# Row statistics of x shared between VectorE and ScalarE, the second source tile from VectorE, eight warming products in place of ten

## The reference

```python
h = jnp.maximum(_layernorm(x, axis=-1), 0.0)      # m, v = mean(x), var(x); (x - m) / sqrt(v + eps)
x = x + _L0_gnn_ref(h, edge_index, ...)           # three edge convolutions, concat @ Wf + bf
h = jnp.maximum(_layernorm(x, axis=-1), 0.0)
x = x + _L1_gnn_ref(h, edge_index, edge_weight, 625, ...)
```

## Time and profile before

| | us |
|---|---|
| three runs | 111.28, 110.65, 111.09 |
| median | 111.09 |
| the profiled execution, whole | 111.21 |
| its span, first to last instruction | 109.4 |

### The profile page before, as it was taken

The page is one execution under the profiler, slowest core; times in us unless marked ns, Lnnn a source line. Parts: engine busy times, 40 slices in busy tenths (PEclk is TensorE's granted clock), DMA queues, the critical chain, the costliest instruction groups (busy, mean ns, idle before and its releaser), DMA issues.

```text
span 109.4 us, 2712 instructions
## 1 busy us (share of the span) xinstructions
PE 98.6 (90%) x1050; PEld 91.8 (84%) x1050; DVE 87.9 (80%) x257; ACT 63.8 (58%) x154; POOL 20.8 (19%) x27
## 2 busy tenths in 40 slices
PE   0395999979999999999999999999999999999950
PEld 0333898867799989999999999999999999999840
DVE  2589999999999998999953599940999989808960
ACT  1595999998699989302858133557513153423540
POOL 7200000000000059100399920192000000000000
PEclk9999999999999999999999999999999999999999
DMA  1984930000030000000050200000000000000035
GB/s 28 260 186 93 328 115 0 0 6 3 3 99 0 6 0 9 6 0 3 0 192 13 88 0 0 6 0 0 0 6 0 0 0 0 0 0 6 0 76 158
DMA packets 7008, 4.63 MB, mean 42 GB/s; under 512 B 2175, under 2 KB 6994, under 8 KB 6994
## 3 DMA queue, kind: packets, MB, share of 16 engines
q1 hardware_dynamic: 6068, 3.68, 12.4%
q10 hardware_dynamic: 926, 0.75, 2.6%
HBM read 3.79 MB, written 0.64 MB: 40 GB/s over the span
## 4 chain that ended last, share of the span: by engine, by line
PE 72%; DVE 17%; DMA 5%; issue 1%; ACTq 1%; ACT 0%; DVEq 0%
PE bank L1385 14%; PE bank L1286 12%; PE bank L1142 12%; PE bank L1143 11%; PE bank L1144 11%; DVE src_hot L591 8%; DMA x_in<-in_x_dram 5%; PE bank L1216 4%; PE bank L1423 2%; PE bank L1363 2%; DVE stats L544 2%; DVE stats L864 1%; PE bank L1468 1%; DVE x_in L895 1%; DVE dst_hot L587 1%
## 5 line engine op out<-in xcount | busy, mean ns | idle before, releaser
L591 DVE TENSOR_SCALAR src_hot<-node_id,edge_cols 125x626 f16<-125x626 f16 x77 | 23.6, 379 | 0.0
L1286 PE MATMUL bank<-dst_hot,src_hot 125*128 125x84 f16 (+6 forms) x505 | 20.1, 195 | 1.3 <-DVE src_hot L591 1.1
L1286 PEld LDWEIGHTS bank<-dst_hot,src_hot 125*128 125x128 f16 x505 | 18.8, 98 | 2.8 <-DVE src_hot L591 1.8
L1385 PE MATMUL bank<-counts,u_lo 125*128 125x312 f32 (+3 forms) x60 | 16.7, 308 | 0.0
L1068 ACT ACTIVATE h_hi<-pre 128x312 fp32r<-128x312 f32 (+1 forms) x12 | 5.6, 466 | 16.4 <-DVE pre L757 16.4
L1385 PE MATMUL bank<-counts,u_hi 125*128 125x312 f32 (+3 forms) x48 | 14.0, 307 | 0.0
L1143 PE MATMUL bank<-wf_hi,h_lo 128*125 128x256 f32 x40 | 11.3, 281 | 0.0
L1142 PE MATMUL bank<-wf_hi,h_hi 128*125 128x256 f32 x40 | 11.3, 281 | 0.0
L1144 PE MATMUL bank<-wf_lo,h_hi 128*125 128x256 f32 x40 | 11.2, 281 | 0.0
L1385 PEld LDWEIGHTS bank<-counts,u_lo 125*128 125x128 f32 (+1 forms) x60 | 11.0, 189 | 0.0
L1003 ACT ACTIVATE parts<-bank 125x250 f32<-125x250 f32 x25 | 10.2, 411 | 0.0
(11 more groups left out here) (144 smaller groups left out, 250.0 us busy)
## 6 DMA issues: line engine op xcount, KB each, us to landing
raw<-in_L_gnn_W_dram SPq DMA_DIRECT2D x3, 512.0 KB, 6.6
x_in<-in_x_dram ACTq DMA_DIRECT2D x1, 560.0 KB
raw<-in_L_gnn_Wf_dram SPq DMA_DIRECT2D x1, 512.0 KB, 3.7
out_dram<-x_in SPq DMA_DIRECT2D x2, 168.0 KB
wf<-in_L_gnn_Wf_dram SPq DMA_DIRECT2D x1, 256.0 KB, 7.6
raw<-in_L_gnn_Wf_dram SPq DMA_DIRECT2D x1, 256.0 KB, 2.7
raw<-in_L_gnn_W_dram SPq DMA_DIRECT2D x1, 256.0 KB, 2.7
out_dram<-x_in SPq DMA_DIRECT2D x2, 112.0 KB
```

Of the source, the lines that this page charges most:

```text
L591: dve.tensor_scalar(src_hot[:, t % RING, 0:IDS], node_id[:, 0:IDS], edge_cols[:, 0, t:t + 1], None, ALU.is_equal).then_inc(src_hot_vector, 1)
L1286: return pe.matmul(built[s][:, :, n0:n0 + n], src_hot[:, t % RING, BLK * s:BLK * s + P], dst_hot[:, c, :, j // 2, c0:c0 + n, j % 2], start ...
L1385: ins = pe.matmul(bank[KF * h + f][:, 0:e - a], u[0:n, k, P * f:P * (f + 1)], counts[0:n, k, a:e], start=False, stop=(k == NB - 1 and u is ...
```

## The change

Three edits.

- VectorE computes the statistics of blocks 0 to 2 only (VECTOR_STATS). ScalarE computes those of blocks 3 and 4 (SCALAR_STATS) after its tile 0: for each a Copy of the block scaled by D^-1.5 with a running sum along the row (`accum_out`), which gives mean / sqrt(D), and then, for each, a Square of (mean - x) / sqrt(D), again with a running sum, which gives the variance. Both write their elementwise result to `h0`, which is overwritten later. The square root waits for both engines. `shift` is then computed by two instructions, one for each group of blocks, and ScalarE waits for both.
- SCALAR_EARLY is (0,): tile 4 goes to VectorE. VectorE makes tile 2 ahead of its wait for the square root.
- `keep_warm(10)` becomes `keep_warm(8)`.

```diff
-SCALAR_EARLY, SCALAR_NEXT, SCALAR_LATER = (0, 4), (22, 27), {0: (34, 38), 1: (52,), 2: (71,)}
+SCALAR_EARLY, SCALAR_NEXT, SCALAR_LATER = (0,), (22, 27), {0: (34, 38), 1: (52,), 2: (71,)}
...
+VECTOR_STATS, SCALAR_STATS = (0, 1, 2), (3, 4)
...
             dve.wait_ge(x_loaded, 32)
-            for b in range(NB):
+            for b in VECTOR_STATS:
                 moments_of(b)
-            variances(range(NB))
+            variances(VECTOR_STATS)
             dve.wait_ge(edge_cols_ready, 1)
             source_tile(1)
-            scale_shift(range(NB), norm_ready)
-            for t in range(2, TILES):
+            source_tile(2)
+            stds[0] += 1
+            dve.wait_ge(std_ready, stds[0])
+            step.add(dve.reciprocal(rstd[0:BLK, 0:NB], rstd[0:BLK, 0:NB]))
+            step.wait()
+            for blocks, by in ((VECTOR_STATS, -1.0), (SCALAR_STATS, -math.sqrt(D))):
+                lo, hi = blocks[0], blocks[-1] + 1
+                dve.scalar_tensor_tensor(out=shift[0:BLK, lo:hi], in0=moments[0:BLK, lo:hi, 0], scalar=by,
+                                         in1=rstd[0:BLK, lo:hi], op0=ALU.mult, op1=ALU.mult).then_inc(norm_ready, 1)
+            for t in range(3, TILES):
...
+            act.wait_ge(x_loaded, 32)
+            for b in SCALAR_STATS:
+                nc.scalar.activation(h0[:, b, :], x_in[:, b, :], ACT.Copy, scale=D ** -1.5,
+                                     accum_out=moments[0:BLK, b, 0:1]).then_inc(row_mean_ready, 1)
+            for i, b in enumerate(SCALAR_STATS):
+                act.wait_ge(row_mean_ready, i + 1)
+                nc.scalar.activation(h0[:, b, :], x_in[:, b, :], ACT.Square, bias=moments[0:BLK, b, 0:1],
+                                     scale=-D ** -0.5, accum_out=moments[0:BLK, b, 1:2]).then_inc(row_variance_ready, 1)
+            act.wait_ge(row_variance_ready, len(SCALAR_STATS))
             root(rstd[0:BLK, 0:NB], moments[0:BLK, 0:NB, 1])
-            act.wait_ge(norm_ready, 1)
+            act.wait_ge(norm_ready, 2)
...
-            keep_warm(10)
+            keep_warm(8)
```

More of the change, by code:

```diff
@@ L326, in gnn_kernel @@
         variance_ready = sem("variance_ready")
+        row_mean_ready = sem("row_mean_ready")
+        row_variance_ready = sem("row_variance_ready")
         std_ready = sem("std_ready")
```

## The result

Over 20 executions of each, the changed kernel takes 111.56 us in the median and the kernel before 111.03. The ratio is 1.0049, 95% interval 1.003 to 1.0067: 0.53 us slower.

The account below looks back on a forecast made before the run. VectorE's source tiles were taken to bound the kernel until 22.61 us, then TensorE. VectorE's saving and the wait for ScalarE's square root gave +0.22 on 111.21, 111.43; as a median 111.3 us, range 110.5 to 112.0.

Parts of the forecast that it names:

- What bounds the kernel: Before 22.61 us VectorE's stream of source tiles sets the pace, with 0.7 us of room on TensorE; after it TensorE.
- VectorE's sum: VectorE's work before deviations changes by -0.83 + 0.29 + 0.08 = -0.46 us, but a wait for ScalarE's square root follows.
- the tiles' net cost: Tile 4 comes to VectorE for 0.29 us; tile 2 moved ahead of the wait fills 0.16 us of idle time.
- When the square root can start: ScalarE's four activations from 7.13 us end at 8.64; with four sum reads the square root starts at 9.46.
- a = 0.20: Cost in us of bringing each of ScalarE's four running sums to memory, taken as not hidden in the overlap.
- a reciprocal before 9.6: Sign against the forecast: VectorE's reciprocal, at 9.64 us in the kernel before, starting earlier than 9.6 us.
- Free sums: Rival on ScalarE: the running sums cost nothing, deviations move by -0.57 us, median 110.5 us; chance 0.12, nearly free included.
- Dear sums: Rival on ScalarE: each sum read costs 0.30 us, deviations move by +0.63 us, median 111.7 us; chance 0.13.
- another table: Rival on ScalarE: Square needs another activation table, two loads add 2.57 us, median 113.9 us; chance 0.03.
- The two products: TensorE's two warming products left out, taken as fast ones of 0.21 us each, gain or cost nothing.
- the cover that was named: TensorE's 0.7 us wait for a source tile at 22.61 us, said to absorb delays on TensorE before it.
- the displacement: Shift of the start of VectorE's deviations, 10.53 us before the change, which moves the end: forecast +0.22 us.

Follow-up runs that it names:

- after: The changed kernel with all three edits, against the kernel before: median 111.56 us against 111.03, ratio 1.0049.
- late_x_after: The changed kernel with the transfer of x issued some 2.5 us later, after the copy of the edge weights; ratio to the kernel before 1.0321.
- after_again: The changed kernel run once more, unchanged, beside the kernel before: 111.57 us against 110.93, ratio 1.0045.

## Why the prediction was right or wrong

**The time and the range.** 111.3 was forecast, 111.56 measured; the range 110.5 to 112.0 and the largest chance, within 0.5%, hold it. That 111.3 came so near is in part luck: the mechanism that the forecast rests on was worth +0.06 us and not +0.22, and most of what was measured is a term that it doesn't have.

**What bounds the kernel.** Right. In every trace with x at its usual place tile 33 on VectorE ends TensorE's last long wait near 22.2 to 22.6, and the span ends 98.7 to 99.0 us after deviations start. What was wrong is the start of the path: in after it comes over ScalarE's tile 0, and not over x.

**VectorE's sum.** Right: tile 1 starts 1.28 us after the statistics where 1.24 were summed, deviations start 1.29 after the square root where 1.30 were, and the tiles' net cost is 0.11 where it was 0.13.

**When the square root can start.** This step was off, in two terms of opposite sign. The four reads were sized at a = 0.20 each; they measure 0.10 (0.40 between Copies less 0.305), the lower of the bounds from the rows, because a read does hide in the overlap. That the Trainium skill's page "ScalarE: Activation LUTs" gives back-to-back activations an overlap of about 93 ns, under "What ACT_TABLE_LOAD costs", agrees with it. This takes 0.4 us off. The start was set at x's landing, 7.13, for both engines, as in the one trace at hand. In the other traces VectorE starts its statistics at 6.65 to 7.01, so x lands at least 0.1 to 0.5 earlier. VectorE's old order profits from that and ScalarE, held by tile 0, doesn't: a lag of 0.18 to 0.31. This gives 0.2 to 0.3 back. Forecast +0.22, measured +0.06. The prediction had named a reciprocal before 9.6 as a sign against itself. It came at 9.35, mostly because everything started 0.3 earlier; it is 2.52 us after the statistics, where the forecast makes it 2.66.

**Free sums.** Fell: each is an instruction of 0.19 us. The reading of the Trainium skill's page "ScalarE activation tables: per-element evaluation and per-set limits" by which a sum is free isn't borne out here. **Dear sums** fell as well, and **another table**: no table load stands among ScalarE's rows between the Copies and the square root.

**The two products.** Costed at nothing. In the changed kernel that can't be told from the truth (109.34 with eight, 109.39 with ten). In the kernel before it was wrong by 0.3 us of mean span, for a reason that no trace caught. The two left out were taken as two fast ones; tile 0's piece comes 3.13 us after the first product in after and 3.42 in after_again, where all eight were slow, against 3.08 in the forecast. And the cover that was named, 0.7 us of wait at 22.6, didn't help where the clock did fall, since the loss in `late_x_after` went over ScalarE.

**What was left out.** The time outside the span was taken as the same 1.8 us in both. It is 2.19, 0.38 us more, and carries most of the loss. Against the 25 executions of the kernel before beside `after_again`, the means differ by 0.57 us: 0.38 outside and 0.20 in the span. Of the 0.20 the displacement would be about 0.06; the rest is long executions without a known cause, and the whole is no larger than what means of a dozen spans can differ by. Semaphores and the sums as such are ruled out; instructions off the path move it; what sets its size, and whether it lies before the first or behind the last instruction, stays open.

## What to carry to other kernels

Before a time between two engines is summed, ask which of several nearly equal arrivals is last in most executions: here x landed 0.1 us after ScalarE was free in the one trace at hand, and at least 0.18 before it in all five such traces of the changed kernel. Work moved off the bounding engine is worth only as much as the wait that takes its place leaves over; one block on ScalarE freed VectorE by 0.22 us, two blocks by nothing, in both cases with tile 4 taken over. And take time less span over many executions before a difference of a few tenths is explained by the path.

## What the runs showed of the hardware

- A running sum is a separate read of 0.19 us on ScalarE, 0.10 of it in the spacing of independent activations; the last before a wait counts with 0.22 (8.80 to 9.02).
- The time outside the span is a property of the program: 1.80 to 1.87 us in five kernels, 1.95 to 2.36 in the seven others, with no one added thing that explains it. Within one kernel it varied by 0.15 where it was 1.8 (1.75 to 1.90 in 83 executions of the kernel before) and by 0.5 where it was 2.2 (1.92 to 2.41 in after).
- In the kernel before TensorE's products stood 0.43 us apart until 7.91 and 0.21 from 8.43 on the earlier trace rows, so it rose to 2.4 GHz 2.6 to 3.1 us after the first of them; in four other traces it had not risen at the end of 4.47 us of products. After idle stretches of 2.40 and 1.39 us with 0.32 us of work between them the granted clock was 0.50 (1.2 GHz) for some 6.8 us. In after, one idle stretch of 1.40 us left it at 1.00.
- The mean granted clock of an execution counts the stretch behind TensorE's last product too: 0.992 in after, where no product ran at the lower clock after the rise.
